# Perceiver layer on one core: squares moved ahead of the first exponentials, a second maximum moved between low thirds, and a tail cut in halves with its gate ahead of the normalised rows

## The reference

```
x = x + xattn(ctx, layernorm(x))     # 16 heads of 64; keys and values of ctx AND of the latents; rmsnorm on q and k; softmax over 1088
x = x + attn(layernorm(x))           # causal over a "sequence" of the two batch rows
x = x + ffn(layernorm(x))            # gated by entmax15

# ffn, on x normalised:
a  = entmax15(layernorm(x @ proj))   # 16 values per row; sort, cumulative sums, square root, threshold, square
g1 = a @ C1;  h = ((x,1) @ Win1 * g1) @ Wout1.T;  h = gelu(h)
g2 = a @ C2;  y = ((h,1) @ Win2 * g2) @ Wout2.T
```

## Time and profile before

| what | value |
| --- | --- |
| median of 3 runs | 232.57 us (232.32 to 232.83) |
| the profiled execution, own time | 233.34 us |
| its span, first to last instruction | 231.4 us |
| PE busy | 220.6 us, 95% of the span |
| DVE, ACT, POOL busy | 152.0, 154.9, 80.2 us |
| mean granted TensorE clock | 1.000 |

### The profile page before, as it was taken

The page is one execution under the profiler, slowest core; times in us unless marked ns, Lnnn a source line. Parts: engine busy times, 40 slices in busy tenths (PEclk is TensorE's granted clock), DMA queues, the critical chain, the costliest instruction groups (busy, mean ns, idle before and its releaser), DMA issues.

```text
span 231.4 us, 4188 instructions
## 1 busy us (share of the span) xinstructions
PE 220.6 (95%) x1446; PEld 190.8 (82%) x1446; DVE 152.0 (66%) x347; ACT 154.9 (67%) x340; POOL 80.2 (35%) x131
## 2 busy tenths in 40 slices
PE   7899999999989999999999999999999998999884
PEld 6556778887778888989888989899999987899773
DVE  2699899998778786776866755566766661303431
ACT  2868777979885968776676567778787755314151
POOL 5188897861592837445160500000000010000300
PEclk9999999999999999999999999999999999999999
DMA  6590134200000000000000899700000000000000
GB/s 184 151 317 32 47 122 175 68 25 0 23 0 3 1 4 0 0 3 0 0 0 3 256 428 328 177 3 0 0 4 0 1 3 0 0 3 0 0 3 23
DMA packets 11252, 13.80 MB, mean 60 GB/s; under 512 B 1592, under 2 KB 9952, under 8 KB 10976
## 3 DMA queue, kind: packets, MB, share of 16 engines
q1 hardware_dynamic: 10680, 11.97, 16.6%
q10 hardware_dynamic: 552, 1.58, 1.9%
HBM read 13.15 MB, written 0.13 MB: 57 GB/s over the span
## 4 chain that ended last, share of the span: by engine, by line
PE 65%; DVE 21%; ACT 5%; issue 4%; DMA 2%; POOL 2%; ACTq 0%; POOLq 0%; DVEq 0%
PE banks L1307 19%; PE banks L1157 14%; PE banks L1216 8%; PE banks L1248 8%; PE banks L1447 5%; DVE small L902 4%; DVE sk L914 4%; PE banks L1321 3%; DMA wraw<-in_L_xattn_Wkv 2%; PE banks L1250 2%; ACT knT L632 2%; PE banks L1370 2%; PE banks L1474 2%; DVE small L871 1%; DVE raw L865 1%
## 5 line engine op out<-in xcount | busy, mean ns | idle before, releaser
L937 DVE TENSOR_TENSOR ptl<-banks,pth 128x512 fp32r<-128x512 f32 (+1 forms) x48 | 26.8, 558 | 24.2 <-ACT pth L668 23.2
L1307 PE MATMUL banks<-xnh,pth 128*128 128x256 f32 x128 | 37.6, 294 | 0.1
L1307 PE MATMUL banks<-xnh,ptl 128*128 128x256 f32 x128 | 36.2, 283 | 0.0
L1307 PE MATMUL banks<-xnl,pth 128*128 128x256 f32 x128 | 36.2, 283 | 0.0
L515 POOL TENSOR_TENSOR small<-small 128x16 f32<-128x16 f32 x7 | 20.4, 2915 | 32.1 <-DVE small L909 32.1
L668 ACT ACTIVATE pth<-banks 128x512 fp32r<-128x512 f32 (+1 forms) x48 | 23.7, 495 | 10.6 <-PE banks L1157 9.5
L615 ACT ACTIVATE sk<-banks 128x512 f32<-128x512 f32 x36 | 20.7, 602 | 12.1 <-PE banks L1216 11.6
L902 DVE TENSOR_REDUCE small<-sk 128x8 f32<-128x512 f32 x36 | 23.6, 678 | 5.9 <-ACT sk L615 5.9
L914 DVE TENSOR_TENSOR sk<-banks,small 128x512 f32<-128x512 f32 x36 | 23.0, 680 | 6.6 <-POOL small L515 6.5
L495 POOL COPY sp<-sp 128x64 f32<-128x64 f32 x16 | 3.8, 238 | 62.8 <-ACT sp L649 62.7
L1157 PE MATMUL banks<-ident,sp 128*128 128x128 f32 x144 | 24.2, 279 | 1.1 <-ACT sp L649 1.1
(11 more groups left out here) (193 smaller groups left out, 478.0 us busy)
## 6 DMA issues: line engine op xcount, KB each, us to landing
knT<-in_L_attn_qkv_kernel SPq DMA_DIRECT2D x1, 3072.0 KB, 12.4
raw<-in_ctx SPq DMA_DIRECT2D x16, 128.0 KB, 2.3
knT<-in_L_xattn_Wq SPq DMA_DIRECT2D x1, 1024.0 KB, 6.8
wv<-in_L_xattn_Wkv ACTq DMA_DIRECT2D x1, 1024.0 KB, 4.9
wout_sb<-in_L_xattn_Wout SPq DMA_DIRECT2D x1, 1024.0 KB, 5.8
knT<-in_L_attn_out_kernel SPq DMA_DIRECT2D x1, 1024.0 KB, 15.2
wraw<-in_L_xattn_Wkv ACTq DMA_DIRECT2D x1, 512.0 KB, 5.0
wraw<-in_L_xattn_Wkv SPq DMA_DIRECT2D x1, 512.0 KB, 5.3
```

Source lines behind the costliest of these rows:

```text
L937: nc.vector.tensor_tensor(ptl[:, j0:j1, :], banks[:, t3_bank(u, c), 0:(j1 - j0) * P].rearrange("p (j r) -> p j r", j=j1 - j0), pth[:, j0:j ...
L1307: nc.tensor.matmul(banks[:, u_bank(u), 0:D], p_[:, j, :], x_, start=(j == 0 and i == 0), stop=False)
```

## The change

It edits five places.

1. **Unit 0, ACT.** `squares(11, 0)` moves ahead of `exponentials(0)`, and `squares(11, 1)` right behind it, from between `keys_out` and the second third.
2. **Unit 0, DVE and PE.** On DVE both `key_norm2` and `key_clamp` stand ahead of the first low third, and `logits_max(1)` moves between the first and the second low third. For it PE issues the third part of `logits(1)` with the other two.
3. **Last unit.** `mix_out`, the transposes and `mixT_out` go in halves of 128 columns; the second half's copy is DVE's (`uT_last`), the banks are 3 and 4. One `keep_clock` matmul less.
4. **Second attention's input.** L1080 goes in two halves; the second half's copy to `hT3` is DVE's. One `keep_clock` matmul less.
5. **Feed-forward.** Centred rows, transposes and copies (both ACT) in halves. `tail["t1"]` is made by POOL, behind the gate's inverse root, and no longer by DVE. PE issues its transposes after 10 dummy matmuls, and `z1` just ahead of the gate's transpose. ACT takes the gate's square root ahead of the copy of the normalised rows and of `z1`, and loads the Gelu table behind the gate's square. In the entmax the support is counted from `root >= cs - k*zs` and no longer from `tau <= zs`, so that the count no longer hangs on two products.

```diff
             unit_high(1)
+            squares(ITEMS_A + 1, 0)
             exponentials(0)
+            squares(ITEMS_A + 1, 1)
...
                     key_norm2(i + 1, 0)
-                    probs_low(u, 0)
                     key_norm2(i + 1, 1)
                     key_clamp(i + 1)
+                    probs_low(u, 0)
+                    logits_max(u + 1)
                     probs_low(u, 1)
-                    logits_max(u + 1)
                     probs_low(u, 2)
...
-                nc.scalar.activation(un[:, :], banks[:, u_bank(u), 0:D], ACT.Copy, scale=rinv[:, u:u + 1]).then_inc(un_ready, 1)
+                for cols in ((slice(0, P), slice(P, D)) if u == UNITS - 1 else (slice(0, D),)):
+                    nc.scalar.activation(un[:, cols], banks[:, u_bank(u), cols], ACT.Copy,
+                                         scale=rinv[:, u:u + 1]).then_inc(un_ready, 1)
...
+            dve.wait_ge(utl_ps, 2)
+            dve.wait_ge(o_ps, u)
+            nc.vector.tensor_copy(uT[:, 1, :], banks[:, 4, 0:P]).then_inc(uT_last, 1)
...
-            nc.vector.scalar_tensor_tensor(tail["t0"], tail["t1"], t_rstd, rows[:, 1, :], ALU.mult, ALU.add).then_inc(h_ready, 1)
+            for c in range(DC):
+                half = slice(c * P, (c + 1) * P)
+                nc.vector.scalar_tensor_tensor(tail["t0"][:, half], tail["t1"][:, half], t_rstd, rows[:, 1, half], ALU.mult,
+                                               ALU.add).then_inc(h_ready, 1)
+            dve.wait_ge(hT_ps, 2)
+            nc.vector.tensor_copy(hT3[:, 1, 0:2, :], banks[:, 4, 0:P].rearrange("p (s i) -> p s i", s=2)).then_inc(hT_ready, 1)
...
+            pool.wait_ge(t_rs, 1)
+            pool.wait_ge(f_ready, DC)
+            nc.gpsimd.tensor_scalar(tail["t1"], tail["t0"], t_rstd, 0.0, ALU.mult, ALU.add).then_inc(t1_ready, 1)
...
-            dve.wait_ge(t_rs, 1)
-            dve.wait_ge(f_ready, 1)
-            nc.vector.tensor_scalar(tail["t1"], tail["t0"], t_rstd, None, ALU.mult).then_inc(f_ready, 1)
...
+            mark(nc.vector.tensor_tensor(gap, cs, zk, ALU.subtract))
             dve.wait_ge(t_rs, 2)
+            mark(nc.vector.tensor_scalar(kr, kinv, e_rstd, None, ALU.mult))
+            dve.wait_ge(dchain, own[0])
+            dve.wait_ge(root_ready, 1)
+            mark(nc.vector.scalar_tensor_tensor(tmp, cs2, 0.0, gap, ALU.add, ALU.is_ge, accum_out=supp))
+            mark(nc.vector.tensor_tensor(cs, cs, cs2, ALU.subtract))
+            taus_at = own[0]
             mark(nc.vector.tensor_scalar(zz, raw_e, zsort[:, 0:1], e_rstd, ALU.subtract, ALU.mult))
-            dve.wait_ge(root_ready, 1)
-            link(nc.vector.tensor_tensor(cs, cs, cs2, ALU.subtract))
-            link(nc.vector.tensor_tensor(cs, cs, kinv, ALU.mult))
-            mark(nc.vector.tensor_scalar(cs2, cs, e_rstd, None, ALU.mult))
-            link(nc.vector.tensor_tensor(tmp, cs, zs, ALU.is_le))
-            link(nc.vector.tensor_reduce(supp, tmp, AX.X, ALU.add))
-            link(nc.vector.scalar_tensor_tensor(tmp, kk, supp, cs2, ALU.is_equal, ALU.mult, accum_out=taus))
+            dve.wait_ge(dchain, taus_at)
+            link(nc.vector.tensor_tensor(kr, cs, kr, ALU.mult))
+            link(nc.vector.scalar_tensor_tensor(tmp, kk, supp, kr, ALU.is_equal, ALU.mult, accum_out=taus))
             nc.vector.tensor_scalar(zz, zz, taus, 0.0, ALU.subtract, ALU.max).then_inc(a_ready, 1)
```

More of the change, by code:

```diff
@@ L282, in perceiver_layer @@
         f_ready = sem("f_ready")
+        t1_ready = sem("t1_ready")
         fT_ps = sem("fT_ps")
@@ L832, in _ @@
             nc.scalar.activation(tail["z1"], banks[:, 3, 0:P], ACT.Identity, bias=bcols[:, 0:1]).then_inc(z1_ready, 1)
-            act.wait_ge(delta_ready, 1)
-            nc.scalar.activation(cs2, cs2, ACT.Sqrt).then_inc(root_ready, 1)
-            nc.scalar.activation(warm[:, 1:2], warm[:, 0:1], ACT.Gelu)
             act.wait_ge(aT_ps, 1)
             nc.scalar.activation(tail["aT"][0:E, :], banks[0:E, 4, 0:P], ACT.Square).then_inc(aT_ready, 1)
+            nc.scalar.activation(warm[:, 1:2], warm[:, 0:1], ACT.Gelu)
             act.wait_ge(g_ps, 2)
@@ L1101, in _ @@
             dve.wait_ge(y2_ps, 1)
-            nc.vector.tensor_scalar(tail["t0"], banks[:, 2, 0:D], banks[:, 2, D:D + 1], None,
-                                    ALU.subtract).then_inc(f_ready, 1)
+            for c in range(DC):
+                half = slice(c * P, (c + 1) * P)
+                nc.vector.tensor_scalar(tail["t0"][:, half], banks[:, 2, half], banks[:, 2, D:D + 1], None,
+                                        ALU.subtract).then_inc(f_ready, 1)
             stats(banks[:, 2, 0:D], t_mvv, t_st).then_inc(t_mv, 1)
-            dve.wait_ge(t_rs, 1)
-            dve.wait_ge(f_ready, 1)
-            nc.vector.tensor_scalar(tail["t1"], tail["t0"], t_rstd, None, ALU.mult).then_inc(f_ready, 1)
             dve.wait_ge(e_ps, 1)
@@ L1311, in mix_transposed @@
             def mix_transposed(u):
+                if u == UNITS - 1:
+                    for c in range(DC):
+                        pe.wait_ge(un_ready, u + c + 1)
+                        transposes(banks[:, 3 + c, :], lambda _: un[:, c * P:(c + 1) * P],
+                                   1).then_inc(utl_ps, 1)
+                    return
                 pe.wait_ge(un_ready, u + 1)
@@ L1320, in values @@
                 for c in range(DC):
+                    if u == UNITS - 1 and c == 1:
+                        pe.wait_ge(uT_last, 1)
                     last = nc.tensor.matmul(banks[:, u_bank(u), 0:P], wv[:, c, g * P:(g + 1) * P], uT[:, c, :], start=(c == 0),
@@ L1375, in _ @@
                     probs_transposed(0, 0)
-                    logits(1, 0)
-                    logits(1, 1)
+                    for part in range(3):
+                        logits(1, part)
                     probs_transposed(0, 1)
@@ L1402, in _ @@
                     pe.wait_ge(w1T_ready, u - w1T_first)
-                logits(u + 1, 2)
+                if u > 0:
+                    logits(u + 1, 2)
                 mix(u)
@@ L1433, in _ @@
             pe.wait_ge(same_ready, 1)
-            keep_clock(8, 3)
-            pe.wait_ge(h_ready, 1)
-            transposes(banks[:, 1, :], lambda c: tail["t0"][:, c * P:(c + 1) * P], DC).then_inc(hT_ps, 1)
+            keep_clock(7, 3)
+            for c in range(DC):
+                pe.wait_ge(h_ready, c + 1)
+                transposes(banks[:, (1, 4)[c], :], lambda _: tail["t0"][:, c * P:(c + 1) * P], 1).then_inc(hT_ps, 1)
             nc.tensor.matmul(banks[:, 2, D:D + 1], ident[:, :], t_mvv[:, 0:1], start=False, stop=False,
@@ L1479, in _ @@
             keep_clock(2, 7)
-            pe.wait_ge(f_ready, 1)
-            transposes(banks[:, 0, :], lambda c: tail["t0"][:, c * P:(c + 1) * P], DC).then_inc(fT_ps, 1)
-            pe.wait_ge(fT_ready, 1)
+            for c in range(DC):
+                pe.wait_ge(f_ready, c + 1)
+                transposes(banks[:, (0, 4)[c], :], lambda _: tail["t0"][:, c * P:(c + 1) * P], 1).then_inc(fT_ps, 1)
+            keep_clock(1, 7)
             pe.wait_ge(w_tail["c"], 48)
```

63 lines of the change are left out of this document (41 added, 22 removed).

## The result

The changed kernel takes 231.09 us (median of 4 runs, 230.81 to 231.45), the kernel before 232.53 us (4 runs, 232.32 to 232.83). The ratio is 0.9937 with a 95% interval of 0.9922 to 0.9951, that is 1.1 to 1.8 us faster. The forecast was 231.3 us.

What follows compares the result with a forecast made beforehand. PE's almost unbroken matmul chain was taken to bound the middle, a row of short steps across engines the tail. 0.16 + 0.30 + 0.13 + 0.66 = 1.25 us off the 232.57 median gave 231.3 us; range 230.8 to 232.3.

Steps and rivals of the forecast that it cites:

- Unit 0: First unit: exponentials start 0.17 late, yet PE takes up unit 1 at 66.43, not 66.59; 0.16 us gained.
- Last unit: Scaled copy to value matmuls: with halves the second pair of passes starts earlier; 0.30 us gained.
- Attention's input: Second attention's input in halves: PE starts at 200.38 to 200.40, not 200.53; 0.13 us gained, 0 to 0.2.
- Gate values: Feed-forward, centred rows in halves: values there 0.32 earlier, DVE free, so the sort starts 0.49 us earlier.
- Entmax: Feed-forward, sort to gate's transpose: one product less ahead of the root, shorter row behind it; 0.37 us earlier, 0.2 to 0.5.
- POOL in the way: Feed-forward: POOL's normalised rows and DVE's last steps ahead of the root collide; root taken as 0.20 us late.
- the other case: Feed-forward: DVE's subtraction waits for the end of POOL's instruction plus 0.15, making the root 0.44 us late.
- The cap: Feed-forward, PE and ACT order: `z1` work keeps the gate's square from starting before 221.80; at most 0.72 of 0.86 comes through.
- The table load: Behind the gate's square: 1.28 us plus 0.20 warm activation on ACT, hidden before the first Gelu with 0.4 to spare.
- The halves pay: Rival, chance 0.13, claimed the opposite: in the tail, extra instructions and hand-overs eat the halves' saving; 0.26 us gained, 232.3 us.
- POOL's instruction takes 0.49 and not 0.74: Rival, chance 0.18: in the feed-forward POOL's instruction takes 0.6 to 0.74, DVE's subtraction waits for all; 0.75 us gained, 231.8 us.
- the rival's mechanism: Rival, chance 0.07: holes on PE ahead of the second attention halve the granted clock; 3 us of it would give 234.3.

Runs made afterwards that it cites:

- the squares alone: The kernel before with only ACT's two squares moved, ahead of and behind the first exponentials; 232.21 us, ratio 0.9978.
- the whole version: The changed kernel with the last unit's scaled copy, transposes, copies and dummy matmul count as before; 231.47 us, ratio 0.9954.
- its own experiment: The changed kernel with L1080, its copy and the dummy matmul count ahead of the transposes as before; 231.17 us, ratio 0.9954.
- the kernel with the maximum alone: The kernel before with only DVE's and PE's order in unit 0 changed, ACT's squares where they were; 234.35 us, ratio 1.0074.
- two kernels without that hole: The changed kernel with normalised rows on DVE again, 231.62 us, and the changed kernel with the old entmax arithmetic, 231.46 us.

## Why the prediction was right

**Size and sign.** 231.3 forecast, 231.09 measured; 1.25 us forecast, 1.35 by the stretches of the trace. That the two sums are so near is in part luck: unit 0 gave 0.25 more than forecast, the four other parts together 0.15 less.

**Unit 0: right in kind, mis-sized, 0.16 forecast, 0.41 measured.** The step that failed is "the square takes 0.61 alone and about 0.59 in a row, so they start at about 58.55, 0.17 late". It set the square behind the end of the keys' copy, while ACT starts an instruction some 0.1 ahead of the recorded end of the one before: it started 0.95 behind the copy's start (55.88, 56.83) and the exponentials 0.51 behind it. The hold-up was 0, which the squares alone showed. With it fell "every ACT step behind it moves by 0.17": the second third's copy came 0.08 late (5.37 behind the maximum's start, 5.29 before). And ACT started the second exponentials 0.1 ahead of the end of its last copy, not at it (62.84 + 1.05, 63.79). With the recorded wait of 0.35 for the maximum gone and this 0.1 on top, they came 0.41 earlier in spite of the 0.08. That the second edit needs the first was not in the prediction; the runs show it (1.07 lost without, 0.10 won with).

**Last unit: right,** 0.30 forecast, 0.27 measured, gone again in the whole version. The copy of 128 columns with its scale took 0.36 in the mean, as forecast.

**Attention's input: half,** 0.13 forecast, 0.07 measured (0.06 by its own experiment). The second half's copy took the forecast 0.29, but it started 1.03 behind the first half's start and not 0.98 (199.97 - 198.99), and PE followed 0.15 behind its end and not 0.12: the hand-overs were set too short.

**Gate values: right,** 0.49 forecast, 0.44 measured.

**Entmax: right in size behind the root, 0.37 forecast in all, 0.32 measured without the lock** (4.07 before, 3.75 with POOL's instruction away), 0.31 of it behind the root (forecast 0.28). "Ahead of the root one product is taken out of the row (0.09 to 0.1)" failed: the kernel without any `t1` on POOL takes 2.26 from sort to root, before 2.27. The product did leave the row, but the instruction behind it started 0.11 after the scan that it waited for (217.36, 217.47), where the product had needed 0.04. Likewise the count started 0.11 behind the root (218.54, 218.65), where the first instruction of before had needed 0.03. Both stand behind two waits; that this is the cause is argued and not shown, and in the first case DVE was also busy with another product until 217.43.

**POOL in the way: near in size, 0.20 forecast, 0.16 measured, but by the other case.** The step that failed is "I take 0.20, since POOL has to start up before it reads", by which the subtraction gets in ahead and only the clip waits. POOL's instruction took 0.49 (forecast 0.48) and began 0.16 ahead of the subtraction; the subtraction waited and ended 0.01 behind it, and the clip kept its 0.18. The instruction ahead, L1160, started 0.10 before POOL's and kept its 0.23. So the case that held is the one forecast at 0.44, the subtraction waits for POOL's end plus 0.15. It cost less since the 0.15 wasn't there, POOL began 1.67 behind the sort and not 1.72, and the subtraction was due 0.1 later than forecast. That the 0.20 came near is luck. The Trainium skill ("SBUF — State Buffer", section "Who interferes with whom") says that a DVE instruction with two SBUF inputs contends with a GpSimd instruction that reads SBUF. The trace agrees: 0.34 inside POOL's instruction and 0.18 away from it.

**The cap: not reached.** The last dummy pass ahead of the gate's transpose was issued at about 219.7 and DVE's clip ended at 219.75, so PE's queue would have been free either way; the gate's transpose started 0.06 behind the clip, the hand-over of before. The forecast had PE's queue free 0.04 ahead of the gate. ACT was nearer to it: its copy of `z1` (L852) ended at 220.14, and the gate's square started at 220.13. Its chain is the forecast's: from the end of POOL's instruction to the start of that copy it is 1.71 us (218.06, 219.77), 1.68 in the forecast. In the kernel with POOL's rows ahead of the statistics the copy again ended at the square's start (220.28, 220.25); there the ten dummy matmuls hold the transposes up. So hardly more than 0.1 us saved behind the root would reach the square. That is argued from the rows; no run here tests it.

**The table load: hidden, as forecast.** ACT was free at 221.9, and the first Gelu waited 0.51 for PE.

**Rivals.** The halves pay. POOL's instruction takes 0.49 and not 0.74. The clock stayed at 1.00 after the change, but the rival's mechanism is real: in the kernel with the maximum alone, 0.50 followed a hole of 1.8 us in unit 0.

## What to carry to other kernels

Compare stretches that begin and end at the same work: two profiled executions differed by 1 us ahead of anything that was changed, while the stretches repeat within 0.02. When an instruction is put into an engine's wait, count its start interval and not its duration; 0.5 us of ACT's work fitted into 0.41 of recorded idle time at no cost, because it overlaps the instruction ahead of it. Of two reorderings on two engines that are worth 0.41 us together, one gave 0.31 alone and the other lost 1.07 alone, so try them both ways before one is judged. A total that comes out right doesn't clear its terms: here one was 0.25 short, and another was near by the wrong case.

## What was not expected of the hardware

- A hole of 1.8 us on PE was followed, in the profiled execution and by its mean clock in one more of six, by a granted clock of 0.50 for about 3.4 us, which made unit 0 1.4 us longer; the fall came 1.2 us after PE had resumed work. With dummy matmuls in the hole the profiled execution stayed at 1.00. Three executions of two kernels without that hole had the same mean clock of 0.993.
- A 128x16 subtraction on DVE took 0.34 instead of 0.18 inside a 128x256 instruction of POOL, while a one-input 128x16 instruction (L1149, 0.24) was not touched by the same POOL instruction. Another one-input 128x16 instruction, the clamp of the sums, was: 0.39 and 0.72 instead of 0.17 inside POOL's two-input instructions of 128x256. What sets the two apart was not tested.
- The start of DVE's first maximum lies between 56.01 and 57.06 us in the profiled executions of these kernels, though nothing ahead of it was changed. Most of it is there by ACT's first copy of the key weights, which starts between 4.64 and 5.80, when their DMA has landed. What makes that vary is open.
